# The part ahead of the scan loop rebuilt (one-pass statistics, second norm by identity, convolution from PSUM, casts on ScalarE, routing ahead of turn 1), and tokens and b2 added in the final sums

## The reference

```
xn  = layernorm(x)                                     # no weights
h   = layernorm(xn) * norm_w + norm_b                  # the second norm
x_ssm, z = split(h @ Win)                              # 256 + 256 channels
x_ssm = silu(causal_conv4(x_ssm) + conv_b)
dt  = softplus(x_ssm @ dt_w + dt_b);  Bt = x_ssm @ Bp;  Ct = x_ssm @ Cp     # 64 states
state = state * exp(-dt * exp(A_log)) + dt * x_ssm * Bt;  y = sum_s state * Ct   # scan over tokens
s   = xn + ((y + x_ssm * D) * silu(z)) @ Wout
# feed-forward on xn: 2 shared experts on all tokens, top 2 of 8 routed experts
x_rms = xn * rsqrt(mean(xn^2) + eps)
ffn = xn + shared(x_rms) + sum_k gate_k * (gelu(x_rms @ W1_e + b1_e) @ W2_e + b2_e)
out = x + s * silu(ffn)
```

## Time and profile before

| | us |
|---|---|
| median of 3 runs | 1844.28 (1843.21 to 1849.92) |
| profiled execution, its own time | 1847.7 |
| its span, first to last instruction | 1845.9 |

### The profile page before, as it was taken

How to read it: one execution, slowest core, us unless ns; L and a number is a source line. 1 busy time by engine, 2 the same in 40 slices (tenths; PEclk the granted TensorE clock), 3 DMA queues, 4 the chain that set the end, 5 groups by cost and what they waited for, 6 DMA issues and landing times.

```text
span 1845.9 us, 42152 instructions
## 1 busy us (share of the span) xinstructions
PE 1589.4 (86%) x12756; PEld 790.5 (43%) x12756; DVE 1725.2 (93%) x1913; ACT 1360.6 (74%) x2504; POOL 1371.3 (74%) x675
## 2 busy tenths in 40 slices
PE   1778659999999999999999999988988889888887
PEld 1544334444444444444444444443434334443343
DVE  6798559999999999999999999999999999999996
ACT  3476748878777868787878777787777687687871
POOL 5036547777777768776777777778989899888985
PEclk9688769999999999999999999999899999899998
DMA  8435565556555665567554655575456555545542
GB/s 236 148 124 187 169 161 119 127 125 175 132 126 125 150 151 126 124 146 169 120 125 125 176 125 126 124 160 129 95 120 146 138 121 103 125 118 130 129 88 64
DMA packets 202208, 249.44 MB, mean 135 GB/s; under 512 B 25939, under 2 KB 104221, under 8 KB 201949
## 3 DMA queue, kind: packets, MB, share of 16 engines
q1 hardware_dynamic: 198020, 239.78, 54.2%
q0 software_dynamic: 4096, 8.40, 1.5%
HBM read 204.00 MB, written 43.66 MB: 134 GB/s over the span
## 4 chain that ended last, share of the span: by engine, by line
PE 29%; issue 25%; DVE 20%; POOL 13%; DMA 5%; ACT 4%; DVEq 2%; SPq 1%; POOLq 0%; ACTq 0%
DVE arena L1151 11%; POOL arena L663 10%; PE ps L1329 10%; PE ps L1343 8%; DVE ps L1141 7%; DMA x_rms_by_expert<-arena,slots 4%; PE ps L1417 2%; ACT arena L883 2%; PE ps L1315 2%; POOL x_rms_by_expert L630 2%; PE ps L1393 1%; SPq L328 1%; POOL pick L587 1%; ACT arena L889 1%; DMA u_scratch<-arena 1%
## 5 line engine op out<-in xcount | busy, mean ns | idle before, releaser
L663 POOL TENSOR_TENSOR arena<-arena 128x1024 f32<-128x1024 f32 x512 | 1202.7, 2362 | 322.3 <-DVE arena L1151 286.3
L1151 DVE TENSOR_TENSOR_SCAN arena<-arena,ps 128x512 f32<-128x512 f32 x1024 | 1176.1, 1201 | 54.7 <-PE ps L1329 37.8
L883 ACT ACTIVATE arena<-arena,neg_A 128x512 f32<-128x512 f32 (+1 forms) x1024 | 671.7, 713 | 87.6 <-DVE arena L1151 86.8
L1343 PE MATMUL ps<-arena,ident 64*64 64x512 f32 x4096 | 569.4, 628 | 3.0 <-POOL arena L663 2.8
L1329 PE MATMUL ps<-arena 128*64 128x128 f32 x6144 | 437.8, 287 | 128.7 <-DVE arena L1151 119.5
L1329 PEld LDWEIGHTS ps<-arena 128*64 128x64 f32 x6144 | 342.2, 141 | 448.8 <-DVE arena L1151 286.6
L1141 DVE TENSOR_TENSOR ps<-arena,ps 128x512 f32<-128x512 f32 x640 | 406.0, 680 | 7.1 <-PE ps L1315 6.4
L889 ACT ACTIVATE arena<-ident,b_turned 128x128 f32<-128x128 f32 x768 | 242.7, 388 | 0.0
L1343 PEld LDWEIGHTS ps<-arena,ident 64*64 64x64 f32 x4096 | 110.6, 134 | 160.2 <-issue 160.2
L630 POOL DMA_INDIRECT x_rms_by_expert<-arena,slots x64 | 69.9, 1091 | 127.6 <-DVE slots L1096 89.2
L1315 PE MATMUL ps<-b_parts,pick 120*128 120x512 bf16 x320 | 124.0, 387 | 13.0 <-DVE arena L1151 12.5
(11 more groups left out here) (166 smaller groups left out, 957.1 us busy)
## 6 DMA issues: line engine op xcount, KB each, us to landing
arena<-c_scratch SPq DMA_DIRECT2D x128, 1024.0 KB, 8.7
arena<-w_routed_scaled SPq DMA_DIRECT2D x40, 256.0 KB, 5.9
arena<-in_L_ffn_W_r_dram SPq DMA_DIRECT2D x40, 256.0 KB, 8.5
arena<-w_shared_tiles SPq DMA_DIRECT2D x128, 64.0 KB, 8.0
x_rms_by_expert<-arena SPq DMA_DIRECT2D x1, 5120.0 KB, 22.4
arena<-x_rms_by_expert SPq DMA_DIRECT2D x40, 128.0 KB, 7.2
routed_by_expert<-arena SPq DMA_DIRECT2D x40, 128.0 KB, 8.3
sz_scratch<-arena SPq DMA_DIRECT2D x8, 512.0 KB, 4.6
```

The costliest lines, as they stand in the source:

```text
L663: nc.gpsimd.tensor_tensor(products[:, i % RING, :, :], states[:, i % 2, :, :], c_rows[:, i // CG, i % CG, :].unsqueeze(1).broadcast_to((P, ...
L883: nc.scalar.activation(decay[:, 2 * i + h, :], dflat[:, ds(slot + h * L, L)], ACT.Exp, scale=aflat[:, ds(col, 1)]).then_inc(s["decay_ready ...
L1151: vector.tensor_tensor_scan(states[:, i % 2, h, :], decay[:, m, :], ps[bank][:], 0.0, ALU.mult, ALU.add).then_inc(s["scanned"], 1)
L1343: ins = mm(y_ps[r][HP * h:HP * h + HP, :], ident[q, q], products[q, slot, h, :], start=False, stop=False, skip_group_check=True)
```

## The change

- **Statistics.** bn_stats on each of 32 groups of 128 tokens replaces sums and squares; the even and odd halves are combined by small operations. xn is made by 32 tensor_scalar operations with the mean and the reciprocal. The second norm follows from the first: xn has mean 0 and variance v / (v + eps), so h is xn times one more factor.
- **Moved between engines.** rms_tok's product and the scaling of W1 go to GpSimd; rms_tok gets a place of its own. The x_rms copies go to ScalarE, and their transposes stand after project_in(1). The convolution reads the projection from PSUM, with operations shortened at the left edge; pad is gone. The three casts of B's parts go to ScalarE (the first in softplus_parts, the others in split_b behind silu_x).
- **Softplus.** relu and abs are taken from PSUM, and one table set, loaded once, serves abs, exp and ln. neg_A is made in the first softplus_parts.
- **Routing.** place_tokens stands ahead of turn 1, with its counts on TensorE between the rms transposes. The scatter has three in flight. GpSimd drains ahead of the scatter, and waits for gates_stored after it, as the transposed gates now lie where the products do.
- **pick** is 120x40, and its column is read 128 times by a broadcast access.
- **Sums.** open_ffn is gone; add_xn_b2 adds xn and b2 in begin_final and in the last group, and the gates and xn for it are loaded with the other data of a final.

```diff
--- before.py
+++ after.py
...
-        pick = sb("pick", [3 * SQ, SQ, P], BF16)
+        pick = sb("pick", [3 * SQ, SQ], BF16)
...
-        x_tok, xn_tok, square_tok, h_tok = tok[0], tok[1], tok[2], tok[3]
+        x_tok, xn_tok, h_tok, rms_tok = tok[0], tok[1], tok[3], tok[5]
...
-        rms_tok = w1_stage[:, 0:TF].rearrange("p (j c) -> p j c", c=C)
+        gates_all = w1_stage[0:E, 0:TF]
...
+            store_turn(1, 1)
+            for b, odd in turns(sp):
+                store_turn(b, odd)
...
+            def load_gates(f):
+                sp.dma_start(gates_in[0:E, :], gate_d[:, f * L:(f + 1) * L]
+                             ).then_inc(s["final_loaded" if f < NB - 1 else "last_gates_loaded"], 16)
+
...
+                sp.dma_start(xn_final, xn_d[:, f * L:(f + 1) * L]).then_inc(s["final_loaded"], 16)
+                load_gates(f)
...
-                                        pattern=[[-1, SQ], [0, P]], channel_multiplier=1).then_inc(m, 1)
+                                        pattern=[[-1, SQ]], channel_multiplier=1).then_inc(m, 1)
...
+            for k in range(2):
+                j = slice(k * NT // 2, (k + 1) * NT // 2)
+                pool.wait_ge(s["rms_scale_made"], k + 1)
+                nc.gpsimd.tensor_tensor(rms_tok[:, j, :], xn_tok[:, j, :], bc3(stats[:, 7, j], C), ALU.mult
+                                        ).then_inc(s["rms_made"], 1)
+            pool.wait_ge(s["w1_staged"], 32)
+            for g_col, a, n in ((g_routed_col, 0, E), (g_shared_col, E, ES)):
+                nc.gpsimd.tensor_scalar(w1_stage[:, a * H:(a + n) * H], w1_stage[:, a * H:(a + n) * H], g_col, None,
+                                        ALU.mult).then_inc(s["w1_scaled"], 1)
+
...
+            pool.drain().then_inc(s["product_ready"], 2 * CG)
...
+            pool.wait_ge(s["gates_stored"], 16)
...
+                for h in range(NH):
+                    nc.scalar.activation(dt_raw[:, h, :], ps[4 + h][:], ACT.Relu, bias=dt_b_cols[h])
+                nc.scalar.preload_act_table_set("natural_log_exp_and_others")
+                for h in range(NH):
+                    ins = nc.scalar.activation(exp_abs[:, h, :], ps[4 + h][:], ACT.Abs, bias=dt_b_cols[h])
+                lnk(ins, 1)
                 nc.scalar.activation(exp_abs, exp_abs, ACT.Exp, scale=-1.0).then_inc(s["exp_made"], 1)
+                act.wait_ge(s["c_b_projected"], b + 1)
+                act.wait_ge(s["b_c_dt_u_stored"], b * (16 * N_SDT) + 16 * N_SDT)
+                nc.scalar.copy(b_new[:, 0, :], ps[6][S:S + SD, :]).then_inc(s["b_first_made"], 1)
+                nc.scalar.copy(c_new, ps[6][0:S, :]).then_inc(s["c_copied"], 1)
                 act.wait_ge(s["exp_made"], b + 1)
                 nc.scalar.activation(log_w, exp_abs, ACT.Ln, bias=1.0).then_inc(s["log_made"], 1)
-                act.wait_ge(s["c_b_projected"], b + 1)
-                act.wait_ge(s["b_c_dt_u_stored"], b * (16 * N_SDT) + 16 * N_SDT)
-                nc.scalar.copy(c_new, ps[6][0:S, :]).then_inc(s["c_copied"], 1)
+                if isinstance(b, int) and b == 0:
+                    link0(nc.scalar.activation(neg_a[:], neg_a[:], ACT.Exp))
+                    nc.scalar.activation(neg_a[:], neg_a[:], ACT.Copy, scale=-1.0)
                 act.wait_ge(s["bt_projected"], b + 1)
                 at = b * (SE * TPB) if isinstance(b, int) else act.snap(b * (SE * TPB))
                 nc.scalar.copy(bt_flat[:, ds(at, SE * TPB)].rearrange("p (e c) -> p e c", c=TPB),
                                ps[7][:, 0:TPB * SE].rearrange("p (c e) -> p e c", c=TPB)).then_inc(s["bt_copied"], 1)
 
-            pad(0)
+            def split_b(b):
+
+                act.wait_ge(s["b_rest_made"], b * 2 + 1)
+                nc.scalar.copy(b_new[:, 1, :], b_rest).then_inc(s["b_second_made"], 1)
+                act.wait_ge(s["b_rest_made"], b * 2 + 2)
+                nc.scalar.copy(b_new[:, 2, :], b_rest).then_inc(s["b_split"], 1)
+
+            def link0(ins):
+                ins.then_inc(s["neg_a_made"], 1)
+                act.wait_ge(s["neg_a_made"], 1)
+
             silu_z(0)
             silu_x(0, 0)
             act.wait_ge(s["scores_projected"], 1)
             nc.scalar.activation(scores.rearrange("p j e -> p (j e)"), ps[4][:, 0:NT * E], ACT.Sigmoid
...
+            silu_z(1)
+            for b in range(NB):
+                act.wait_ge(s["rms_turned"], b + 1)
+                nc.scalar.copy(x_rms[:, b * L:(b + 1) * L], ps[4 + (b + 1) % 3][:]).then_inc(s["x_rms_copied"], 1)
+            softplus_parts(0)
+            silu_x(1, 1)
+            split_b(0)
             for b, odd in turns(act):
-                pad(b)
                 silu_z(b)
                 softplus_parts(b - 1)
                 silu_x(b, odd)
+                split_b(b - 1)
...
+                for one in range(j.start, j.stop):
+                    ins = vector.bn_stats(parts_of_x[:, one, :], x_tok[:, one, :])
+                link(ins)
+                means, squares = ([parts_of_x[:, j, 3 * odd + n] for odd in range(2)] for n in (1, 2))
+                vector.tensor_tensor(stats[:, 0, j], means[0], means[1], ALU.add)
+                vector.tensor_tensor(stats[:, 3, j], means[0], means[1], ALU.subtract)
+                link(vector.tensor_tensor(stats[:, 1, j], squares[0], squares[1], ALU.add))
+                vector.tensor_scalar(stats[:, 0, j], stats[:, 0, j], 0.5, None, ALU.mult)
+                link(vector.scalar_tensor_tensor(stats[:, 3, j], stats[:, 3, j], 0.25, stats[:, 3, j], ALU.mult, ALU.mult))
+                link(vector.scalar_tensor_tensor(stats[:, 1, j], stats[:, 1, j], 1.0 / C, stats[:, 3, j], ALU.mult, ALU.add))
...
+                link(vector.tensor_tensor(stats[:, 4, j], stats[:, 1, j], stats[:, 2, j], ALU.mult))
+                link(vector.tensor_tensor(stats[:, 3, j], stats[:, 4, j], stats[:, 2, j], ALU.mult))
+                vector.tensor_scalar(stats[:, 4, j], stats[:, 3, j], LN_EPS, None, ALU.add)
+                vector.tensor_scalar(stats[:, 5, j], stats[:, 3, j], F32_EPS, None, ALU.add).then_inc(s["variance_made"], 1)
+                for one in range(j.start, j.stop):
+                    ins = vector.tensor_scalar(xn_tok[:, one, :], x_tok[:, one, :], stats[:, 0, one:one + 1],
+                                               stats[:, 2, one:one + 1], ALU.subtract, ALU.mult)
+                ins.then_inc(s["xn_made"], 1)
...
+                dve.wait_ge(s["xn_made"], k + 1)
+                vector.reciprocal(stats[:, 6:8, j], stats[:, 6:8, j]).then_inc(s["rms_scale_made"], 1)
+                dve.wait_ge(s["rms_scale_made"], k + 1)
...
-                dve.wait_ge(s["conv_input_copied"], b * NH + 2 * NH)
+                dve.wait_ge(s["input_projected"], b * 4 + NH)
                 for h in range(NH):
                     dve.wait_ge(s["silu_x_made"], b * NH + (h + 1))
-                    ins = vector.tensor_scalar(conv_out[:, h, :], conv_in[:, h, 0:L], convw_sb[:, h, 0:1], None, ALU.mult)
+                    ins = vector.tensor_scalar(conv_out[:, h, :], ps[h][:], convw_sb[:, h, K - 1:K], None, ALU.mult)
                     for j in range(1, K):
                         k += 1
                         ins.then_inc(s["vector_step"], 1)
                         dve.wait_ge(s["vector_step"], done + k)
-                        ins = vector.scalar_tensor_tensor(conv_out[:, h, :], conv_in[:, h, j:j + L], convw_sb[:, h, j:j + 1],
-                                                      conv_out[:, h, :], ALU.mult, ALU.add)
+
+                        ins = vector.scalar_tensor_tensor(conv_out[:, h, j:L], ps[h][:, 0:L - j],
+                                                          convw_sb[:, h, K - 1 - j:K - j], conv_out[:, h, j:L],
+                                                          ALU.mult, ALU.add)
                     ins.then_inc(s["conv_made"], 1)
 
             def parts_and_dt(b, odd, done):
@@ -1012,23 +1028,20 @@
...
-                dve.wait_ge(s["c_b_projected"], b + 1)
-                dve.wait_ge(s["b_c_dt_u_stored"], b * (16 * N_SDT) + 16 * N_SDT)
-                lnk(vector.tensor_copy(b_new[:, 0, :], ps[6][S:S + SD, :]))
+                dve.wait_ge(s["b_first_made"], b + 1)
+                dve.wait_ge(s["b_split"], b + 1)
                 vector.tensor_tensor(b_rest, ps[6][S:S + SD, :], b_new[:, 0, :], ALU.subtract
                                     ).then_inc(s["b_rest_made"], 1)
-                dve.wait_ge(s["b_rest_made"], b * 2 + 1)
-                lnk(vector.tensor_copy(b_new[:, 1, :], b_rest))
-                vector.tensor_tensor(b_rest, b_rest, b_new[:, 1, :], ALU.subtract).then_inc(s["b_rest_made"], 1)
-                dve.wait_ge(s["b_rest_made"], b * 2 + 2)
-                vector.tensor_copy(b_new[:, 2, :], b_rest).then_inc(s["b_split"], 1)
-
                 dve.wait_ge(s["exp_made"], b + 1)
+                dve.wait_ge(s["b_c_dt_u_stored"], b * (16 * N_SDT) + 16 * N_SDT)
```

(63 more changed lines are left out.)

157 lines of the change are left out of this document (45 added, 112 removed).

## The result

The changed kernel takes 1868.74 us (median of 4 runs, 1854.42 to 1880.62), the kernel before 1845.15 (4 runs, 1843.21 to 1849.92): ratio 1.0126, 95% interval 1.0094 to 1.0159. It is slower by 1.3%, where a gain to 1814 us was predicted (range 1797 to 1830). The profiled execution of it took 1854.42 us (span 1852.7), against 1847.7 (1845.9) before.

A forecast was written before the change was run, and what follows sets the result against it. VectorE was taken to bound the main loop, and a chain over all engines and queues the first 257 us. Gains of 26.5 us before the loop and 3.7 in it made 30.2: 1814 us, range 1797 to 1830.

The forecast's parts named there:

- Part 3: From the end of silu_x(7) to the loop: 6.1 us more gained, 3.1 us lost as GpSimd's first product waits for gates_stored.
- The third in flight is then worth nothing: Scatter beside the turns: done by 191 us, rows asked for at about 209, so its speed was priced at zero.
- F: Rival, chance 0.02: another wait of SP holds the loop's start, so the change gives next to nothing, within 0.5%.
- Part 1: Start of the kernel to the end of turn 1's silu: silu_x(1) ends near 88 us instead of 102.6, 14.6 us earlier.
- no hold: Before the first projection: VectorE's h multiply not held by GpSimd's rms multiplies; one hold of 4.7 us was assumed, bounds 0 and 9.4.
- this SP chain: Before turn 1: GpSimd scales W1, SP stores W1, xn, then silu_z(0), landing near 68 us; silu_z(1) waits for it.
- Part 2: The six turns up to silu_x(7): four of 16.5 us and two of 13.6, 93.2 us in all.
- rival B: Turns: the clock holds at 2.4 GHz in all of them, 11.6 us less, 1802.5 us; chance 0.20.
- hidden, with 2 us to spare: Turns: dt_u's store lands near 9.3 us after silu_x, while ScalarE asks for it at 11.6.
- Part 4: The loop: heads return 15.5 us, seven final groups lose 11 and the last group 0.9; net gain 3.7 us.
- D: Rival, chance 0.12: final groups lose more than the heads return; the loop loses 12 us instead of gaining 3.7, 1830 us.
- E: Rival, chance 0.04 with smaller routing mishaps: slower, as broadcast weight loads over 0.6 us eat the gain; some 1880 us at 0.8.

## Why the prediction was wrong, step by step

The step that failed stands in Part 3: "The third in flight is then worth nothing". I asked only whether the scatter would end in time. It did (167.9 us, "done by 191" was predicted), and for that reason I priced its speed at zero. The price was on the other engines: 44 us (1868.7 - 1824.3), more than the whole forecast gain of 30.2. What I had not asked is what GpSimd's pauses between the issues were good for. The runs put in its place a delay of TensorE's signals, up to 34.7 us, that comes when GpSimd issues without a pause. None of the rivals held it; F, another wait, was looked for only at the loop's start.

With that one constant put back, the profiled execution has a span of 1814.9, so 31.0 less than before, where my sum said 30.2. It is a fast one of six, though: its median is 7.5 us above it, and the timed gain is 1.1%, some 20 us. The terms, in spans:

- **Part 1.** The first projection starts at 38.15 us (predicted 43, or 39 with no hold). There was a hold as the row of 2.40 us had hinted, of 3.0 us (5.32 - 2.29) and not 4.7. That it comes sooner even than 39 has two other terms: xn is made at 26.3 (27.8), and turning and copying end 3.7 us behind the last half (6). W1's scaling takes 13.54 us, beyond my upper bound of 11.8. It ends at 51.5, a microsecond after my 50.5, since it began earlier. silu_z(1) ends its wait at 66.65 (predicted near 68), the scatter starts at 79.8 (79.5), silu_x(1) ends at 90.36 (88). The sum is right within 2.4 us. I had written that this SP chain "eats half of what the statistics give"; that was so, and the order of two stores gives it back.
- **Part 2.** Six turns took 125.2 us, predicted 93.2; with two in flight 95.7 (185.53 - 89.85). The sum is nearly right and its reason is not: with two in flight all six dt groups run at full clock (3.60 to 3.67 us, against 6.62 in the earlier trace rows), which was rival B at 13.6 us a turn, and a turn still takes 15.9. ScalarE waits for the store of u, which I called "hidden, with 2 us to spare":

```profile
ACT arena L771 <- DMA u_scratch<-arena: 9.4, 5, 2.2
```

  SyncE issues three stores of b's parts (2.6 to 3.1 us) between b_split and that store, and b_split now comes last on ScalarE. I counted the store from dt_u alone, and left out what is queued before it.
- **Part 3.** From silu_x(7) to the first scan it took 29.4 us before and 24.5 after: 4.9 gained of 6.1 predicted. The first product comes 19.6 us after the first scan (before 9.7), as GpSimd waits for gates_stored, and groups 0 and 1 take 72.0 us against 68.5: 3.5 lost of 3.1 predicted.
- **Part 4.** VectorE's wait in the group behind a head falls from 2.6 us to 0.6:

```profile
DVE arena L1166 <- PE ps L1349: 0.6, 1, 0.6
```

  That is 2.1 us in the length of the group, as predicted, but only behind four heads; behind the last three it is 0.4, 0.1 and 1.7, and behind the first head it is none. Together 10.6 came back and not 15.5, so this term was too large. Six of the seven final groups lose 1.7 to 2.5 us each (1.6 predicted), as the wait of 1.6 us at state 2 of group 43, shown above, does. So groups 2 to 62 take 1504.1 us, before 1504.2: no net gain, 3.7 predicted. A difference of that size cannot be told from one trace: with the same code for these groups they take 1497.9 (two in flight) to 1506.9 us (drain before every sixth), and with the old code 1504.2 and 1498.8. D (12 lost) was wrong, and E: the broadcast's weight load costs nothing to be seen.

Ledger of the changed kernel: first scan +6.1, groups 0 and 1 +3.5, groups 2 to 62 -0.1, last group -2.7 (36.5 against 39.3; with the same code in it, it takes 36.5 with two in flight and 38.9 with a drain before every sixth) = +6.8 = 1852.7 - 1845.9. It is the fastest of its four executions; the others are 13 to 26 us longer. Only one was traced, so that their stall is longer is likely and not shown.

What stays open: what holds TensorE's signals back while GpSimd issues, and what lets one streak of a dozen go by and another run away. The loop over the turns is part of it. The queues between 130 and 198 us of the changed kernel (packets, MB, share of 16 engines) are

```profile
q1 hardware_dynamic: 3824, 6.94, 28.8%
q0 software_dynamic: 960, 1.97, 8.8%
q14 instruction: 1, 0.01, 0.0%
```

One packet of the queues marked "instruction" in 68 us, at 130.2 us, ahead of the stall: no engine was seen to fetch instructions during it. The Trainium skill (Runtime: NRT & Kernel Launch, Instruction fetch mechanics) says that a taken branch out of the window already held makes an engine fetch by DMA before it goes on. That would fit the smaller loss with the turns written out; but a fetch that is only late would leave its packet at the stall's end, and there is none, so the trace doesn't bear it out and a fetch that could not be asked for isn't excluded.

## What to carry to other kernels

A transfer that is "off the path" still has a rate, and raising the rate of GpSimd's indirect DMAs can hold up everyone who waits for TensorE: ask what an added buffer takes away in pauses, and look for idle times with no releaser while one engine issues at a constant step. Where the profile names no releaser, read in the code which semaphore ends the idle time, and who raises it, before you count the engine as stalled itself. When a store is said to be hidden, count what its queue issues before it, from the event that frees the queue. Order stores by who waits for their landing, not by when they are ready.

## What the runs showed of the hardware that was not expected

- Indirect DMAs of 128 rows that GpSimd issued every 1.27 us, three in flight, went with TensorE's semaphore updates up to 34.7 and 30.1 us late, VectorE's and ScalarE's at most 0.01, and so with idle times of 16 to 29 us on VectorE, ScalarE and TensorE. A memset of 0.55 us between two issues, or a drain every twelfth, was enough against the stall.
- SyncE's register operations in the turns, at most 0.06 us in the kernel before, took about 0.7 us ten times in the changed kernel. They did so eight times with the drain before every twelfth and four times with two in flight as well, without a stall, and never without the scatter; so they tell of the issuing and not of the stall.
- VectorE's two-input multiply of 128x2048 takes 2.29 us alone and 5.32 beside GpSimd's multiply; GpSimd's takes 3.6 alone and 5.7 beside it. GpSimd's tensor_scalar needs 13.5 us for 5120 columns, 2.6 ns a column, more than its two-input multiply (1.75 to 2.3).
- In the kernel with two in flight TensorE ran the dt groups of the six turns in 3.60 to 3.67 us, behind idle times of up to 0.94 us (granted clock 1.00). In the changed one it took 5.37 and 5.99 us behind idle times of 3.69 and 25.13: it began at 1.2 GHz (granted clock 0.50 from 166.1 to 168.5 us) and rose within the group.
